# GpSimd reports that a unit has landed after issuing both scatters of the next unit, not between them

## What is computed

```python
def _L1_ffn_ref(x, Wg, W1, b1, W2, b2):      # 8 experts, 2 chosen for each token
    P = jax.nn.softmax(jnp.einsum('bsd,de->bse', x, Wg), axis=-1)
    _, topk_idx = jax.lax.top_k(P, K)
    mask = jax.nn.one_hot(topk_idx, E, dtype=x.dtype).sum(-2)
    P_topk = P * mask
    P_norm = P_topk / (P_topk.sum(axis=-1, keepdims=True) + EPS)
    h = jax.nn.gelu(jnp.einsum('bsd,edf->ebsf', x, W1) + b1[:, None, None, :], approximate=False)
    y_e = jnp.einsum('ebsf,efd->ebsd', h, W2) + b2[:, None, None, :]
    return jnp.einsum('ebsd,bse->bsd', y_e, P_norm)
```

## Time and profile before

| | |
|---|---|
| median of the runs | 453.9 us (452.7 to 454.86, 3 runs) |
| the profiled execution's own time | 452.68 us |
| its span, first to last instruction | 450.9 us |
| TensorE busy | 413.2 us, 92% of the span |
| VectorE, ScalarE, GpSimd busy | 285.3, 213.9, 155.6 us |
| scatters of results (line 707) | 72 issues, 974 ns each |

### The profile page before, as it was taken

How to read it: one execution, slowest core, us unless ns; L and a number is a source line. 1 busy time by engine, 2 the same in 40 slices (tenths; PEclk the granted TensorE clock), 3 DMA queues, 4 the chain that set the end, 5 groups by cost and what they waited for, 6 DMA issues and landing times.

```text
span 450.9 us, 9851 instructions
## 1 busy us (share of the span) xinstructions
PE 413.2 (92%) x2944; PEld 346.0 (77%) x2944; DVE 285.3 (63%) x1137; ACT 213.9 (47%) x525; POOL 155.6 (35%) x215
## 2 busy tenths in 40 slices
PE   7699998999999999999988999888999999999863
PEld 6579777878869779787767879687998999898521
DVE  4869888888888878878867666422344344333217
ACT  3364646565554545543423434334555555555212
POOL 6440015013232340343333012454454555554400
PEclk9989999999999999999999999999999999999988
DMA  7459511253164330132213123412222222222656
GB/s 182 117 117 150 68 39 34 58 155 122 37 186 120 81 85 21 46 82 52 77 51 77 47 51 90 118 55 65 73 70 60 72 71 71 70 71 66 233 189 189
DMA packets 64211, 40.80 MB, mean 90 GB/s; under 512 B 18341, under 2 KB 57129, under 8 KB 64169
## 3 DMA queue, kind: packets, MB, share of 16 engines
q1 hardware_dynamic: 59472, 31.27, 28.8%
q0 software_dynamic: 4352, 8.99, 6.0%
q10 hardware_dynamic: 344, 0.03, 0.1%
HBM read 21.78 MB, written 18.48 MB: 89 GB/s over the span
## 4 chain that ended last, share of the span: by engine, by line
PE 44%; issue 19%; DVE 15%; DMA 8%; SPq 6%; ACT 5%; POOL 1%; DVEq 1%; POOLq 0%; ACTq 0%
PE psB L855 6%; PE psA L1029 5%; PE psB L843 5%; PE psC L1041 3%; DMA ring<-routed 2%; DMA results<-nat,y_to 2%; PE psB L1052 2%; PE psD L972 2%; DMA routed<-send,slot 2%; SPq L490 1%; DVE stats L1325 1%; PE psD L957 1%; PE psC L746 1%; PE psB L845 1%; POOL routed L694 1%
## 5 line engine op out<-in xcount | busy, mean ns | idle before, releaser
L694 POOL DMA_INDIRECT routed<-send,slot x64 | 64.3, 1004 | 129.0 <-DMA routed<-send,slot 59.8
L707 POOL DMA_INDIRECT results<-nat,y_to x72 | 70.1, 974 | 91.8 <-DVE nat L1638 36.5
L1029 PE MATMUL psA<-xuT,w_all 128*128 128x256 f32 x288 | 69.1, 382 | 2.7 <-ACT h1T L1239 2.1
L1239 ACT ACTIVATE h1T<-psA,b1T 128x256 f32<-128x256 f32 x144 | 63.2, 474 | 12.0 <-PE psB L1052 7.8
L1029 PEld LDWEIGHTS psA<-xuT,w_all 128*128 128x128 f32 x288 | 50.5, 190 | 10.8 <-ACT h1T L1239 2.6
L1610 DVE TENSOR_SCALAR xu<-ring 128x256 f32 (+1 forms) x38 | 11.3, 297 | 74.9 <-DMA ring<-routed 65.2
L1041 PE MATMUL psC<-w_all,h1T 128*128 128x128 f32 x464 | 56.9, 276 | 1.0 <-DVE nat L1622 1.0
L1041 PEld LDWEIGHTS psC<-w_all,h1T 128*128 128x128 f32 x464 | 54.1, 192 | 1.7 <-ACT h1T L1239 1.1
L1230 ACT ACTIVATE xuT<-psB 128x256 f32<-128x256 f32 x37 | 14.2, 383 | 62.4 <-PE psB L1019 43.0
L843 PE MATMUL psB<-xnT,w_l 128*128 128x512 f32 x64 | 34.9, 627 | 0.0
L1170 ACT ACTIVATE hg0T<-psB,b1T 128x512 f32<-128x512 f32 x32 | 22.0, 688 | 23.6 <-PE psB L845 23.5
(11 more groups left out here) (289 smaller groups left out, 853.8 us busy)
## 6 DMA issues: line engine op xcount, KB each, us to landing
ring<-routed SPq DMA_DIRECT2D x38, 130.0 KB
inv<-inv_room SPq DMA_DIRECT2D x8, 512.0 KB, 4.2
w_all<-results SPq DMA_DIRECT2D x15, 256.0 KB, 4.7
routed<-ring SPq DMA_DIRECT2D x24, 130.0 KB, 7.7
n_room<-nT SPq DMA_DIRECT2D x8, 256.0 KB
w_all<-in_L_ffn_W_dram SPq DMA_DIRECT2D x1, 2048.0 KB
out_dram<-x_all SPq DMA_DIRECT2D x8, 256.0 KB, 2.3
results<-nat,y_to POOLq DMA_INDIRECT x72
```

The lines of the kernel that those rows point to most:

```text
L694: pool.indirect_dma_start(routed[:, :], bass.IndirectOffsetOnAxis(ap=slot[par][:, c, t:t + 1], axis=0), send[par][:, c, t, :], None).then_ ...
L707: pool.indirect_dma_start(results[:, :], bass.IndirectOffsetOnAxis(ap=y_to[:, par, a:a + 1], axis=0), yw[:, par, a, :], None).then_inc(S[f ...
L1029: last = mm(psA[:, j // 2, (j % 2) * UNIT:(j % 2 + 1) * UNIT], w1_all[:, e, j * P:(j + 1) * P], xuT[:, :], start=True, stop=True)
L1239: f(h1T[:, j, :], psA[:, j // 2, (j % 2) * UNIT:(j % 2 + 1) * UNIT], ACT.Gelu, bias=b1T[:, n:n + 1]).then_inc(S["gelu_ready"], 1)
```

## The change

In `send_results` the wait for the unit before and the raise of `y_landed` leave the loop over the two halves and come behind it. Nothing else differs. The waits, their thresholds and what they guard stay as they are; every unit but unit 0 has one, as before.

```diff
                 wait_on(pool, "yw_ready", u + 1)
                 pool.sem_inc(apart, 1)
                 for a in range(HALVES):
-                    if a and not (isinstance(u, int) and u == 0):
-
-                        pool.wait_ge(S[f"y_sent{1 - par}"], (u + par) * (8 * HALVES))
-                        pool.sem_inc(S["y_landed"], 1)
                     pool.indirect_dma_start(
                         results[:, :], bass.IndirectOffsetOnAxis(ap=y_to[:, par, a:a + 1], axis=0),
                         yw[:, par, a, :], None).then_inc(S[f"y_sent{par}"], 16)
+                if not (isinstance(u, int) and u == 0):
+
+                    pool.wait_ge(S[f"y_sent{1 - par}"], (u + par) * (8 * HALVES))
+                    pool.sem_inc(S["y_landed"], 1)
```

## The result

The changed kernel took 449.02 us (median of 14 runs, 446.9 to 450.65) against 452.85 us for the kernel before in the same comparison (14 runs). The ratio is 0.9921, with a 95% interval of 0.9898 to 0.9943: 3.6 us faster, between 2.6 and 4.6. The forecast was 1.65 us.

The account below looks back on a forecast made before the run. Ring loads stall the loop; three result landings in a row bound the end. Nothing gained or lost elsewhere, 1.65 us gained at the last landing: 452.68 - 1.65 = 451.0 us profiled, 452.2 as median; 8-in-10 range 450.4 to 454.4.

Parts of the forecast that it names:

- The wait moved, the raise later, the loop unharmed: In the loop: the raise of y_landed comes 0.5 us later, VectorE has about 0.8 us to spare, cost nothing.
- the seven held ones: Second scatters in the loop taken to be held by the landing wait; their gaps behind the firsts total 10.2 us.
- The slower rival: In the loop: VectorE waits for y_landed in every unit, 0.73 us for 28 units, 20 us slower, 474; chance 0.03.
- Straight part worth nothing: In the straight part: the moved waits come behind scatters already gone out, cost nothing.
- All stalls count: Rival, in the loop: every held second scatter is on the path, gain 8.1 us, to 445.8; chance 0.04.
- Step 1: At the end: unit 34's second scatter no longer waits for unit 33, starting at 423.15 instead of 425.12.
- step 3: At the end: unit 35's second scatter no longer waits for unit 34, starting at 427.85, 1.71 us earlier.
- Step 4: At the end: the last scatter lands after 2.3 us, at 430.15 instead of 431.79, gain 1.65 us.
- A to B 1.71 us shorter: At the end: from unit 34's first scatter's start to unit 35's second's, 5.97 us forecast against 7.68 before.
- step 2: At the end: unit 35's y_to still needs unit 33's landing, so its first scatter stays at 426.58.
- The whole 1.65 us passes through to the end: In the final sums: TensorE is ready with 2.4 us of cover left, so the end comes 1.65 us earlier.
- The level: Whole kernel: the profiled execution ran 1.2 us below the median of 453.9, so the forecast median is 452.2 us.

Follow-up runs that it names:

- units 8 to 33 alone: New order in the loop's units 8 to 33, old order elsewhere, against the kernel before: 450.94 us, ratio 1.0017.
- the five old ones: Traces with units 34 and 35 in the old order: 7.86 us on average from unit 34's first scatter's start to unit 35's second's.
- the eight new ones: Traces with the new order in unit 35, mostly also 34: 5.47 us on average from unit 34's first scatter's start to unit 35's second's.

## Why the prediction was wrong

- **The wait moved, the raise later, the loop unharmed:** right in the main. The raise came at 1.1 us, and units 8 to 33 alone gave 1.0017. But VectorE waited twice, 0.89 us of it in unit 25, and unit 24's second scatter stayed late: it wasn't held by the landing alone, so the seven held ones and their 10.2 us were misread. The slower rival's price of 20 us stood up when its condition was made true (19 us against before; about 22 against the changed kernel, if ratios of different chips may be set side by side). Its limit was put too far out: a raise that may come as late as 369.7 is 1.3 us behind the first scatter's start at 368.40, not 1.5.
- **Straight part worth nothing:** right (0.9997). **All stalls count:** wrong by the same run as the loop.
- **Step 1 and step 3, the last scatter no longer waits:** right. Step 1 moved nothing else: unit 34's landing came no sooner after A. **Step 4, it lands after 2.3 us:** right, 2.24 in the chain.
- **The size of steps 2 and 3, A to B 1.71 us shorter:** mis-sized, 2.4 us over 13 executions. The last scatter's wait was 2.0 us on average over the five old ones, against 1.71 in the one execution that I read, and the way to unit 35's first scatter was shorter in the new ones by about 0.4 us, for which step 2 had taken one execution's 4.61 us as fixed; in the eight new ones unit 33 landed after 3.7 to 4.4. These landings share the DMA engines with a load, and their length varied from run to run. A price read off one loaded landing should have carried that spread to both sides; I let it work against the gain alone.
- **"The whole 1.65 us passes through to the end":** this step failed, and it is the failure of mechanism. It asked only whether TensorE would be ready and took the 4.0 us of idling as cover. The idling had a price, which the sum put at nothing without a reason: the sums behind them ran at about half the granted clock. Ending the wait sooner gave 0.7 us more over the eight new traces, 0.9 where the clock stayed up. The evidence was in front of me: 3.66 us for four records where two of the same size take 1.02 us.
- **The level:** 452.85 us for the kernel before in 14 runs, where the three runs shown had a median of 453.9. That is 1.05 us of the 3.2 between forecast and result.

The parts come to 3.1 us of 3.6: 2.4 of landings and 0.7 of clock. The remaining half microsecond is inside the interval and isn't explained.

No kernel here beats the changed one beyond its interval: 0.9914, 0.9915, 0.9917, 0.9919 and 0.9921 are the same.

## What to carry to other kernels

Before a wait is called cover, look at the granted clock behind it. Where TensorE idles for some microseconds and then works on the path, shortening the idle time can be worth more than the time that it is shortened by, as here, where 0.7 to 0.9 us came on top. A landing wait between two issues on a queue needn't cost anything: here 26 units of the loop gave nothing, and on the chip where it was tried one scatter, the last, gave as much as both last units. And a landing's price belongs to what else is on the DMA engines at that moment, so moving either of the two moves the price.

## What the runs showed of the hardware

GpSimd's queue ran ahead of its scatters: in the changed kernel, in 30 of 35 units, the raise behind two scatters of 0.97 us each stood 1.0 to 1.1 us behind the entry that released the first, before the second had begun; in the other five it came later, up to 3.8 us. From unit 8 on the raise moved by about 0.5 us, not by the 1.27 us from scatter to scatter. One scatter of 66 KB landed 2.2 to 2.4 us after its start in the stretches without a load, and after 3.0 to 6.3 us beside a load of 2 MB; unit 34's landed 6.6 to 7.6 us after A whether it was issued 1.3 or 2.5 to 3.6 us after it. TensorE ran the same four records in 1.98 us at a granted clock of 1.00 and in 3.4 to 3.7 us at about half, after 4.0 to 4.2 us of idling and, in three traces, after 2.50, 2.57 and 2.75.
